# A macaron block on one core: expert weights copied to a ring and held stationary, biases off TensorE, attention on both row halves with its maxima and query masks on VectorE

## The chip, the core and the metric

The kernel runs on one core of a Trainium2 chip. A core has five engines that run their own instruction streams and meet only through semaphores: TensorE (PE) multiplies matrices and transposes, VectorE (DVE) and ScalarE (ACT) work element by element, GpSimd (POOL) does here a few element-wise steps and issues the indirect DMAs, and SyncE (SP) issues the plain ones. The on-chip memory has 128 partitions; TensorE writes into eight banks of a second memory, from which VectorE and ScalarE read.

The metric is the device time of one launch in microseconds (us), a median over runs.

## The reference

`x` holds 16 sequences of 256 tokens with 128 channels, so 4096 token rows. Everything is float32.

```
x = x + 0.5 * ffn(layernorm(x))
x = x + attention(layernorm(x))
x = x + 0.5 * ffn(layernorm(x))

ffn:   logits = x @ Wg.T + bg                      # 16 experts
       top 2 of them, softmax over the two -> cw
       gu = x @ Wgu[e] + bgu[e]                    # 128 -> 256
       gate, up = gu[::2], gu[1::2]                # min(gate, 7), clip(up, -7, 7)
       gated = (up + 1) * gate * sigmoid(1.702 * gate)
       out = sum over the two: cw * (gated @ Wd[e] + bd[e])

attention: q, k, v = split(x @ W_attn + b_attn), 16 heads of 8
       att = softmax(causal(q @ k.T / sqrt(8)));  y = att @ v
       y @ W_proj + b_proj
```

Both ffn use the same weights. The reference computes all 16 experts and masks; the kernel computes the chosen two.

## The kernel before, in words

**Stages.** The program runs once through: first router, first expert stage, attention with its projections, second router, second expert stage, output. Lines are those of the kernel before.

**Router.** It works on eight groups of four row tiles (512 tokens each, q = 0 to 7). For each: statistics (L853), variances, and one GpSimd power that turns variances into 1/std (the "root", L519). In the first router the root comes twice: for groups 0 and 1 before the first scatter, and one of 24 columns for groups 2 to 7 behind it. Then follow the normalised rows, transposes (L1287) and logits (L1295) on TensorE, the choice of two (L904), the ranks within each expert (L1307 to L1312), the positions (L932), and eight indirect DMAs on GpSimd that scatter the rows into a table sorted by expert (L528), 64 in all. A small table then says which expert each tile of 128 rows belongs to.

**Experts.** 80 tiles of 128 sorted rows are worked in 40 duos of two tiles (10 turns of 4 duos). Step functions are run at fixed distances behind each other: `turn_x` (L1355) transposes the rows, `gate_up` (L1364, L1365) multiplies, `turn_g` (L1373) transposes the gated result, `down` (L1384, L1385) multiplies again. Each product has a second one in front of it, of 3 rows, that adds the bias as three bf16 parts. The token rows are the stationary operand, and the expert's weights are the moving one, addressed through a register that TensorE loads from the tile table. ScalarE evacuates `xT` (L677), the sigmoid (L682), `gT` (L688) and `ysb` (L695); VectorE makes the gate in three operations (L1057, L1059, L1061) after one small one for the targets (L1054); GpSimd stores each duo with two indirect DMAs (L560).

**Attention.** 16 sequences times 4 groups of 4 heads are 64 units; 16 units make a turn of the loop. In unit s TensorE runs `scores(s+2)`, `max_T(s+1)`, `weights(s)` and `weigh_values(s-1)`.

- `scores` first writes the causal mask into the banks (L1125, L1128), then adds 12 products q·k (L1132, L1138), which use 64 of the 128 rows of the array: those of one head slot.
- VectorE takes the row maxima by two reductions (L762, L763), splits them into three bf16 parts (L765 to L771); `max_T` (L1146) transposes them.
- `weights` spreads the negated maxima over the keys (L1158, L1159, `select`), adds the mask (L1161, L1163) and forms the transposed products k·q (L1167, L1171); ScalarE takes the exponential (L594).
- `weigh_values` (L1191) multiplies with the values and a column group of ones, so that each head's denominator comes out beside it. Its two column halves of the array are used by neighbouring products.
- In two of each four units VectorE divides (reciprocal L779 on 128x256 elements, two multiplications L783); in the fourth `project_out` (L1199, L1200) follows and the residual is added (L789). Every eight units there are the projections to q, k and v of the next pair of sequences (L1096 to L1108), the splitting into bf16 parts (L753), the combination of the expert results (L715), and DMAs that stack the parts.

The last turn of attention also carries the first six groups of the second router; groups 6 and 7 come after it.

**What sets the order.** Each engine has its own program with the same sequence of steps; there is no planner. The class `Steps` (L1399) says which extra step falls in which unit, and `expert_pipeline` (L1469) how far the expert steps lie apart. On TensorE `scores` waits until the maxima of the unit two before are finished (`a_max`), since both use banks 0 to 2.

## Time and profile before

| | us |
|---|---|
| median of 3 runs | 1057.16 |
| lowest, highest | 1048.26, 1139.39 |
| span of the profiled execution | 1057.0 |

| engine | busy us | share of the span | instructions |
|---|---|---|---|
| TensorE, products | 842.6 | 80% | 5146 |
| TensorE, weight loads | 524.2 | 50% | 5147 |
| VectorE | 523.3 | 50% | 1733 |
| ScalarE | 283.7 | 27% | 537 |
| GpSimd | 338.3 | 32% | 346 |

A share of busy time is a mean over stages that have different limits, so the span is read in stretches: 0 to 118 first router, 118 to 351 first expert stage, 351 to 389 the way into attention, 389 to 709 its first 48 units, 709 to 786 the last turn up to the first scatter of the second router, 786 to 888 the rest of the last turn, the scatters and the tile table, 888 to 1028 the second expert stage, 1028 to 1057 output.
### The profile page before, as it was taken

How to read it: one execution, taken by the hardware profiler on the slowest of the kernel's cores; microseconds unless marked ns; L12 is line 12 of the kernel's file. 1: busy time of each engine (PE TensorE's matmuls, PEld its weight loads, DVE VectorE, ACT ScalarE, POOL GpSimd, SP SyncE). 2: the span in 40 equal slices, each digit the busy share in tenths (PEclk: the TensorE clock that was granted, in tenths of full speed). 3: DMA queues.
4: the chain of work that ended last, by engine and by line, in shares of the span. 5: the costliest groups of instructions: out<-in, count | busy, mean ns of one | idle time of the engine just before them, and what ended most of it. 6: DMA issues, size and time to landing. Idle time of an engine off the chain costs nothing.

```text
span 1057.0 us, 16653 instructions
## 1 busy us (share of the span) xinstructions
PE 842.6 (80%) x5146; PEld 524.2 (50%) x5147; DVE 523.3 (50%) x1733; ACT 283.7 (27%) x537; POOL 338.3 (32%) x346
## 2 busy tenths in 40 slices
PE   2240599999999249999999999999999633999970
PEld 1230255555555125666566656665666421555540
DVE  6571112212222245867586648677598650333326
ACT  1120122222222003333333223333233211334430
POOL 2677533333333201010101010102115672565560
PEclk9999999999999999998899789989598855999985
DMA  7026111111110152241324114223101125232217
GB/s 232 31 65 95 48 48 48 45 47 47 45 47 27 55 179 89 93 137 45 99 83 143 37 48 134 93 68 103 58 12 39 46 61 74 78 81 80 80 55 238
DMA packets 83348, 82.77 MB, mean 78 GB/s; under 512 B 10374, under 2 KB 74332, under 8 KB 83164
## 3 DMA queue, kind: packets, MB, share of 16 engines
q1 hardware_dynamic: 68508, 55.69, 18.2%
q0 software_dynamic: 10368, 23.15, 7.2%
q10 hardware_dynamic: 4416, 3.16, 1.4%
q8 instruction: 39, 0.64, 0.3%
q14 instruction: 17, 0.14, 0.0%
HBM read 41.92 MB, written 39.99 MB: 78 GB/s over the span
## 4 chain that ended last, share of the span: by engine, by line
PE 69%; DVE 10%; POOL 9%; issue 5%; DMA 4%; ACT 1%; SPq 1%; DVEq 0%; POOLq 0%; ACTq 0%
PE banks L1365 14%; PE banks L1385 8%; PE banks L1191 8%; POOL rows_by_expert L528 7%; PE banks L1364 4%; PE banks L1167 3%; PE banks L1158 3%; PE banks L1384 3%; PE banks L1138 3%; PE banks L1355 2%; PE banks L1373 2%; PE banks L1132 2%; PE banks L1125 2%; PE banks L1161 2%; PE banks L1102 2%
## 5 line engine op out<-in xcount | busy, mean ns | idle before, releaser
L560 POOL DMA_INDIRECT results_by_token<-ysb,goes_to x160 | 153.1, 957 | 221.4 <-ACT ysb L695 193.4
L1054 DVE TENSOR_TENSOR goes_to<-xt,konst_sb 128x2 int32<-128x2 f32 x80 | 12.9, 161 | 308.3 <-ACT sig L682 308.3
L1365 PE MATMUL banks<-w_experts,xT 128*128 x320 | 155.8, 580 | 0.0
L594 ACT ACTIVATE pT<-banks 128x1536 f32<-128x1536 f32 x64 | 92.8, 1451 | 121.1 <-PE banks L1171 121.1
L1191 PE MATMUL banks<-pT,values_spread 128*64 128x256 f32 (+1 forms) x1024 | 113.7, 367 | 0.0
L1385 PE MATMUL banks<-w_experts,gT 128*128 x320 | 103.4, 416 | 0.0
L1191 PEld LDWEIGHTS banks<-pT,values_spread 128*64 128x64 f32 x1024 | 81.0, 150 | 34.9 <-issue 18.8
L528 POOL DMA_INDIRECT rows_by_expert<-values_spread,posi x80 | 77.5, 969 | 40.5 <-issue 23.2
L1355 PE MATMUL banks<-konst_sb,xt 128*128 128x128 f32 x160 | 41.8, 355 | 59.1 <-DMA xt<-rows_by_expert 59.1
L762 DVE TENSOR_REDUCE mraw<-banks 128x4 f32<-128x512 f32 x64 | 44.2, 691 | 79.5 <-PE banks L1146 68.8
L1365 PEld LDWEIGHTS banks<-w_experts,xT 128*128 128x128 f32 x320 | 64.8, 253 | 27.9 <-issue 18.9
L763 DVE TENSOR_REDUCE mraw<-banks 128x4 f32<-128x1024 f32 x64 | 77.7, 1215 | 0.0
L1385 PEld LDWEIGHTS banks<-w_experts,gT 128*128 128x128 f32 x320 | 64.4, 251 | 14.8
L682 ACT ACTIVATE sig<-banks 128x256 f32<-128x256 f32 x80 | 30.6, 383 | 151.6 <-PE banks L1365 151.6
L496 POOL CAST q_parts<-sig 128x512 bf16<-128x512 f32 x7 | 4.2, 604 | 201.7 <-DVE sig L753 201.7
L588 ACT ACTIVATE mT<-banks 12x256 bf16<-12x256 f32 x64 | 23.8, 373 | 151.7 <-PE banks L1146 151.7
L779 DVE RECIPROCAL rsum<-ysum 128x256 f32<-128x256 f32 x34 | 59.4, 1747 | 1.1 <-ACT ysum L601 1.1
L1355 PEld LDWEIGHTS banks<-konst_sb,xt 128*128 128x128 f32 x160 | 28.0, 189 | 60.6 <-issue 58.6
L695 ACT ACTIVATE ysb<-banks 128x256 f32<-128x256 f32 x80 | 30.7, 383 | 96.5 <-PE banks L1385 96.5
L1364 PE MATMUL banks<-bias,ones 3*128 x160 | 53.9, 337 | 0.0
L1158 PE MATMUL banks<-mT,select 12*128 12x256 bf16 x256 | 53.7, 286 | 0.0
L1287 PE MATMUL banks<-konst_sb,values_spread 128*128 128x128 f32 x40 | 11.1, 433 | 49.8 <-DVE values_spread L879 49.8
(180 smaller groups left out, 1429.1 us busy)
## 6 DMA issues: line engine op xcount, KB each, us to landing
xt<-rows_by_expert SPq DMA_DIRECT2D x160, 64.5 KB, 1.9
q_stack<-q_by_part SPq DMA_DIRECT2D x8, 1024.0 KB, 7.2
k_stack<-k_by_part SPq DMA_DIRECT2D x8, 1024.0 KB, 7.2
q_by_part<-q_parts SPq DMA_DIRECT2D x16, 384.0 KB, 3.3
k_by_part<-k_parts SPq DMA_DIRECT2D x16, 384.0 KB, 2.8
yg<-results_by_token POOLq DMA_DIRECT2D x8, 512.0 KB, 5.0
results_by_token<-ysb,goes_to POOLq DMA_INDIRECT x160, 2.2
x_resident<-in_x SPq DMA_DIRECT2D x8, 256.0 KB, 5.3
```

The costliest lines, as they stand in the source:

```text
L528: pool.indirect_dma_start(out=rows_dram, out_offset=bass.IndirectOffsetOnAxis(ap=posi[:, c:c + 1], axis=0), in_=rows_of(f, q)[:, i, k, :], ...
L560: pool.indirect_dma_start(out=results_dram, out_offset=bass.IndirectOffsetOnAxis(ap=goes_to[:, 2 * k + i:2 * k + i + 1], axis=0), in_=ysb[ ...
L594: nc.scalar.activation(pT[:, s % 2, :], banks[:, 3:6, :].rearrange("p a q -> p (a q)"), ACT.Exp, scale=SCALE).then_inc(a_exp, 1)
L762: ch.mark(nc.vector.tensor_reduce(mraw[:, 0, :], bank[0][:, :].rearrange("p (g k) -> p g k", g=GRP), AX.X, ALU.max))
L763: ch.mark(nc.vector.tensor_reduce(mraw[:, 1, :], banks[:, 1:3, :].rearrange("p a (g k) -> p (a g) k", g=2), AX.X, ALU.max))
L779: ch.mark(nc.vector.reciprocal(rsum[:, c], ysum[:, c]))
L1158: nc.tensor.matmul(bank[3 + g // 2][:, g % 2 * T:(g % 2 + 1) * T], select[:, g, :], mT[:, s % 2, :], start=g % 2 == 0, stop=False)
L1191: last = nc.tensor.matmul(bank[6][r:r + HALF, c + kt * P:c + T], of_head, w, start=j == 0 and g < 2 and kt == 0, stop=j == GRP - 1 and g > ...
L1355: last = nc.tensor.transpose(bank[k % 2][:, i * P:(i + 1) * P], xt[:, 2 * k + i, 0:C], ident)
L1364: nc.tensor.matmul(o, ones[0:3, :], bias3[:, bass.ds(e[i], 2 * F)], start=True, stop=False)
L1365: last = nc.tensor.matmul(o, xT[:, k % 2, i * P:(i + 1) * P], w_all[:, bass.ds(e[i], 2 * F)], start=False, stop=True)
L1385: last = nc.tensor.matmul(o, gT[:, k % 2, i * P:(i + 1) * P], w_all[:, bass.ds(e[i] + 2 * F, C)], start=False, stop=True)
```

## The change

**Experts.** ScalarE copies the 384 weight columns of each tile's expert to a ring (`w_tile`, eight places) by an address from a register. TensorE reads fixed addresses, holds the weights (64 columns at a time) and streams the tokens, so `gate_up` gives the result already transposed: `turn_g` and its evacuation are gone. `down` runs in row halves of its output. The 3-row bias products are gone: `evac_x` adds 1.0 to each value, and during the first router `column_sums` and `adjust` change the weights once so that the added ones yield the bias; the bias of `down` is added by VectorE as it evacuates the result, which takes that evacuation from ScalarE. The steps lie further apart: in one slot ScalarE and TensorE work on four duos instead of three.

**Attention.** A head's rows are chosen so that neighbouring groups use different halves of the rows (`slot_of`). `scores` has no mask products. The maxima are taken by eight `tensor_tensor_reduce` that add the mask and reduce, and they are split into two parts instead of three. `scores` now waits for the eight (`a_read`), not for the end of the split. Since two halves of the rows may not write one bank at the same time, `scores` and `weights` wait once in between (`a_s_low`, `a_st_low`). `weigh_values` runs on quarters of the columns. The division is done once for each sequence on 32 denominators: `tokens_first` (4 transposes), a reciprocal of 128x32, one multiplication, `channels_first` (2 transposes), an evacuation by ScalarE, then `project_out` with its bias as one product.

**First router.** The roots come in four groups (`GROUPS`): quads 0, 1, and 2 to 3 before the first scatter, 4 to 7 (16 columns) behind it.

```diff
-EARLY = 2
+GROUPS = ((0, 1), (1, 2), (2, 4), (4, 8))
...
+                def copy_weights(t, k):
+                    n = t * DUOS + k + f * PAIRS
...
+                    beyond_first(act, s_y, n - (DUOS - 1))
+                    for i in range(2):
+                        last = nc.scalar.activation(w_tile[:, 2 * k + i, :], w_all[:, bass.ds(experts[key][k % 2 * 2 + i], EW)], ACT.Identity)
+                    last.then_inc(s_w, 1)
...
-                expert_pipeline(act, evac_x, sigmoid, evac_g, evac_y)
+                expert_pipeline(act, (1, evac_x), (2, sigmoid), (0, copy_weights))
...
+                ch.mark(nc.vector.memset(spare[:, :], 0.0))
+                for g in range(GRP):
+                    for qt in range(QT):
+                        of = bank[0][:, g * P:(g + 1) * P] if qt == 0 else bank[1 + g % 2][:, g // 2 * T:(g // 2 + 1) * T]
+                        lag = kc[:, K_MQ:K_MQ + P] if qt == 0 else kc[:, K_Z:K_Z + T]
+                        last = nc.vector.tensor_tensor_reduce(masked[:, (3 * g + qt) * P:(3 * g + 2 * qt + 1) * P], of, lag, 1.0, NEG * NEG_BELOW, ALU.add, ALU.max, mraw[:, s % 2, qt, g:g + 1])
+                        last.then_inc(a_read, 1)
...
-                ch.mark(nc.vector.tensor_reduce(mraw[:, 0, :], bank[0][:, :].rearrange("p (g k) -> p g k", g=GRP), AX.X, ALU.max))
-                ch.mark(nc.vector.tensor_reduce(mraw[:, 1, :], banks[:, 1:3, :].rearrange("p a (g k) -> p (a g) k", g=2), AX.X, ALU.max))
...
+                ch.mark(nc.vector.reciprocal(rsum[:, :], by_head[:, :, D]))
...
-                ch.mark(nc.vector.reciprocal(rsum[:, c], ysum[:, c]))
...
+                def evac_y(t, k):
+                    e = offsets(t, k)
...
+                    ch.mark(nc.vector.tensor_copy(goes_to[:, 2 * k:2 * k + 2], going[:, 2 * k:2 * k + 2]))
...
+                    for i in range(2):
+                        last = nc.vector.tensor_tensor(ysb[:, k, i, :], bank[6 + k % 2][:, i * C:(i + 1) * C], w_all[:, bass.ds(e[i] + EW, C)], ALU.add)
...
+                expert_pipeline(dve, (2, gate), (4, evac_y), (1, targets), chain=(ch, 3))
...
-                beyond_first(pe, a_max, n)
+                beyond_first(pe, a_read, n * 2 * GRP)
...
-                nc.tensor.matmul(bank[0].rearrange("p (g k) -> p g k", g=GRP), identb[:, :],
-                                 mask_q[:, :].unsqueeze(1).to_broadcast([P, GRP, P]), start=True, stop=False)
...
+                late(1)
+                early(0)
+                early(2).then_inc(a_s_low, 1)
+                late(3)
+                late(0)
+
+                pe.wait_ge(a_s_low, n + 1)
+                early(1)
+                late(2)
+                early(3).then_inc(a_s, 1)
...
+                    for i in range(2):
+                        o, e = bank[6 + n % 2][:, i * 2 * F:(i + 1) * 2 * F], 2 * n + i
+                        nc.tensor.matmul(o, share[0:3, :], bias3[0:3, e * BW:e * BW + 2 * F], start=True, stop=False)
+                        last = nc.tensor.matmul(o, spread[:, :], w_all[:, e * WB:e * WB + 2 * F], start=False, stop=True)
...
+                    for i in range(2):
+                        for which in range(2):
+                            for h in range(2):
+                                at = which * 2 * P + i * P
+                                last = nc.tensor.matmul(bank[2 + k % 2][h * HALF:(h + 1) * HALF, at:at + P],
+                                                        w_tile[:, 2 * k + i, which * F + h * HALF:which * F + (h + 1) * HALF],
+                                                        xT[:, k % 2, i * P:(i + 1) * P], start=True, stop=True)
...
-                expert_pipeline(pe, turn_x, gate_up, turn_g, down)
+                expert_pipeline(pe, (1, turn_x), (2, gate_up), (4, down))
```

The order of TensorE's instructions in the expert loop, before. One duo's share: `turn_g`, `turn_x`, `gate_up`, `down`; ISA rows with a matrix product's line are its register-addressed preparation.

```order
L1373 MATMUL banks<-konst_sb,upc 128x128 [waits s_gated]
L1373 MATMUL banks<-konst_sb,upc 128x128
...
L1355 MATMUL banks<-konst_sb,xt 128x128 [waits s_xt1,s_xt0]
L1355 MATMUL banks<-konst_sb,xt 128x128
...
L1364 ISA [waits s_xT]
L1364 MATMUL banks<-bias,ones 128x256
L1365 ISA
L1365 MATMUL banks<-w_experts,xT 128x256
...
L1384 ISA [waits s_ysb3,s_gT]
L1384 MATMUL banks<-bias,ones 128x128
L1385 ISA
L1385 MATMUL banks<-w_experts,gT 128x128
```

And after the change. `L1487` is `turn_x`, `L1500` is `gate_up`, `L1512` is `down`.

```order
L1487 MATMUL banks<-konst_sb,xt 128x128 [waits s_xt1,s_xt0]
L1487 MATMUL banks<-konst_sb,xt 128x128
L1492 REGISTER_ALU
L1599 REGISTER_ALU [waits s_xT,s_w]
L1500 MATMUL banks<-xT,pT 64x128 [waits s_gated]
L1500 MATMUL banks<-xT,pT 64x128 x7
L1512 MATMUL banks<-pT,row_buf 64x128 [waits s_ysb3,s_gated]
L1512 MATMUL banks<-pT,row_buf 64x128 x3
```

`turn_g`, the 3-row products and the register-addressed weights are gone; eight products of 64 columns stand in place of two of 128 with their bias, and a wait on the copied weights (`s_w`) is new.

TensorE's order in an attention unit, before: `scores`, `max_T`, `weights`, `weigh_values`.

```order
L1125 MATMUL banks<-mask_q,identb 128x512 [waits a_max]
L1128 MATMUL banks<-mask_q,identb 128x2x128 x2
L1132 MATMUL banks<-k_stack,q_stack 128x128 x4
L1138 MATMUL banks<-k_stack,q_stack 128x128 x8
L1146 MATMUL banks<-identb,mparts 12x128 [waits a_max,a_k_rest]
L1146 MATMUL banks<-identb,mparts 12x128
L1158 MATMUL banks<-mT,select 128x256 [waits a_exp,a_mT]
L1159 MATMUL banks<-mT,select 128x128
...
L1161 MATMUL banks<-mask_k,identb 128x2x128 x2
L1163 MATMUL banks<-mask_k,identb 128x512
L1167 MATMUL banks<-q_stack,k_stack 128x256 x4
L1171 MATMUL banks<-q_stack,k_stack 128x128 x4
L1191 MATMUL banks<-pT,values_spread 64x256 [waits a_exp,a_mT]
```

And after. `L1193` and `L1199` are the products of `scores`, `L1218` is `max_T`, `L1234` and `L1238` spread the maxima, `L1243` and `L1247` are the products of `weights`, `L1293` is `weigh_values`.

```order
L1199 MATMUL banks<-k_stack,q_stack 128x256 [waits a_read]
L1193 MATMUL banks<-k_stack,q_stack 128x128 x2
L1199 MATMUL banks<-k_stack,q_stack 128x256 x2
L1193 MATMUL banks<-k_stack,q_stack 128x128 [waits a_s_low]
L1199 MATMUL banks<-k_stack,q_stack 128x256
L1193 MATMUL banks<-k_stack,q_stack 128x128
L1218 MATMUL banks<-identb,mparts 64x128 [waits a_max,a_k_rest]
L1218 MATMUL banks<-identb,mparts 64x128 x3
L1234 MATMUL banks<-mT,select 128x256 [waits a_exp,a_mT]
L1238 MATMUL banks<-mT,select 128x128 x2
...
L1293 MATMUL banks<-pT,by_token 32x256 [waits a_exp]
L1293 MATMUL banks<-pT,by_token 32x256 x3
L1293 MATMUL banks<-pT,by_token 32x128 x4
```

The two mask rows ahead of the scores are gone, the wait `a_max` has become `a_read`, the scores are 8 products in place of 12, and a wait on `a_s_low` stands between the fifth and the sixth.

VectorE's order for the row maxima of a unit, before.

```order
L762 TENSOR_REDUCE mraw<-banks 128x4 [waits a_mTp,a_s]
L763 TENSOR_REDUCE mraw<-banks 128x4
L765 CAST mparts<-mraw 128x2x4 [waits s_vec]
L767 TENSOR_TENSOR mrest<-mraw,mparts 128x8 [waits s_vec]
L769 CAST mparts<-mrest 128x2x4 [waits s_vec]
L771 TENSOR_TENSOR mparts<-mrest,mparts 128x2x4 [waits s_vec]
```

And after (five more pairs of `L799` are left out).

```order
L794 MEMSET spare 128x1 [waits a_s]
L799 ISA by_token,mraw<-banks,konst_sb 128x128
L799 ISA mraw 128x1
L799 ISA by_token,mraw<-banks,konst_sb 128x256
L799 ISA mraw 128x1
...
L799 ISA by_token,mraw<-banks,konst_sb 128x256
L799 ISA mraw 128x1
L804 CAST mparts<-mraw 128x2x4 [waits a_mTp,a_read]
L806 TENSOR_TENSOR mparts<-mraw,mparts 128x2x4 [waits s_vec]
```

Two reductions have become eight instruction pairs, each a main one and a read of its accumulated value, and the four small operations of the split have become two.

## Rows read from the trace of the kernel before

**Rows 1.** Stages by windows: stretch, length, busy time per engine (count), PEclk, DMA share, GB/s.

```profile
118.00:351.00 233.00, 227.88 (x640) 125.71 (x640) 50.07 (x160) 60.67 (x160) 82.11 (x82) 1.00 0.16 44
389.00:709.00 320.00, 307.93 (x2597) 199.61 (x2596) 220.05 (x518) 105.97 (x129) 31.20 (x35) 0.93 0.27 88
709.00:786.00 77.00, 74.08 (x605) 49.57 (x604) 56.99 (x193) 24.53 (x31) 8.57 (x7) 0.84 0.17 56
786.00:888.00 102.00, 58.57 (x494) 41.50 (x493) 62.44 (x259) 23.32 (x31) 63.69 (x65) 0.73 0.25 54
888.00:1028.00 140.00, 135.71 (x640) 79.94 (x640) 50.11 (x160) 53.27 (x160) 75.53 (x79) 0.95 0.27 74
```

**Rows 2.** Groups by line, 160 to 300 (first expert stage): line, engine, names, count | busy, mean | idle.

```profile
L1365 PE MATMUL banks<-w_experts,xT 128*128 x100 | 61.1, 715 | 0.0
```

**Rows 3.** Chain that ended last, 118 to 351, its shares by line.

```profile
by line: PE banks L1365 39.5%; PE banks L1385 23.7%; PE banks L1364 11.1%; PE banks L1355 7.2%; PE banks L1384 7.0%; PE banks L1373 7.0%; DMA results_by_token<-ysb,goes_to 1.9%; issue 1.3%; POOL results_by_token L560 1.2%; DMA xt<-rows_by_e
```

**Rows 4.** Groups by line, 920 to 1000 (second expert stage).

```profile
L560 POOL DMA_INDIRECT results_by_token<-ysb,goes_to x50 | 47.9, 957 | 33.7 <-ACT ysb L695 23.9 <-issue 9.8
L1365 PE MATMUL banks<-w_experts,xT 128*128 x100 | 35.0, 432 | 0.0
```

**Rows 5.** Chain that ended last, 480 to 495: start, us, what; one attention unit.

```profile
483.54 2.81 PE banks L1191 x16
...
491.20 1.50 PE banks L1191 x16
```

**Rows 6.** Timeline of PE, 440 to 447: start, us, line, operands, count; one unit.

```profile
440.97 0.39 PE L1125 MATMUL banks<-mask_q,identb 128*128 128x512 bf16 x1
...
441.51 0.40 PE L1132 MATMUL banks<-k_stack,q_stack 64*128 64x128 bf16 x4
...
442.29 0.28 PE L1146 MATMUL banks<-identb,mparts 128*12 128x128 bf16 x2
442.50 0.28 PE L1158 MATMUL banks<-mT,select 12*128 12x256 bf16 x1
...
443.26 0.39 PE L1161 MATMUL banks<-mask_k,identb 128*128 128x256 bf16 x2
...
446.06 0.39 PE L1125 MATMUL banks<-mask_q,identb 128*128 128x512 bf16 x1
```

**Rows 7.** Groups by line, DVE, 389 to 709 (48 attention units).

```profile
L763 DVE TENSOR_REDUCE mraw<-banks 128x4 f32<-128x1024 f32 x48 | 58.3, 1214 | 0.0
L779 DVE RECIPROCAL rsum<-ysum 128x256 f32<-128x256 f32 x23 | 40.2, 1747 | 0.0
L762 DVE TENSOR_REDUCE mraw<-banks 128x4 f32<-128x512 f32 x48 | 33.2, 692 | 69.6 <-PE banks L1146 59.2 <-PE banks L1138 9.2 <-issue 0.3
...
L715 DVE SCALAR_TENSOR_TENSOR x_resident<-yg,wts,x_resident 128x128 f32 x48 | 13.7, 348 | 0.9 <-DVE x_resident L715 0.9
```

**Rows 8.** Timeline of DVE, 950 to 954: the gate's operations on one duo.

```profile
951.88 0.16 DVE L1054 TENSOR_TENSOR goes_to<-xt,konst_sb 128x2 int32<-128x2 f32 x1 [1.98 <-ACT sig L682]
951.96 0.42 DVE L1057 SCALAR_TENSOR_TENSOR sig<-banks,sig 128x256 f32<-128x256 f32 x1
952.30 0.41 DVE L1059 TENSOR_SCALAR upc<-banks 128x256 f32<-128x256 f32 x1
```

**Rows 9.** Timeline of POOL, 30 to 46 (first router).

```profile
31.42 4.21 POOL L519 TENSOR_TENSOR rstd<-veps,neghalf 128x24 f32<-128x24 f32 x1
42.20 1.03 POOL L528 DMA_INDIRECT rows_by_expert<-values_spread,posi  x1 [6.57 <-DVE posi L942]
43.53 0.96 POOL L528 DMA_INDIRECT rows_by_expert<-values_spread,posi  x1 [0.30 <-issue]
```

**Rows 10.** Timeline of POOL, 780 to 890 (the second router's longest wait).

```profile
814.61 0.96 POOL L528 DMA_INDIRECT rows_by_expert<-row_buf,posi  x1 [8.27 <-DVE posi L942]
```

**Rows 11.** DMA issues of the page: operands, queue, count, KB each, us to landing.

```profile
k_stack<-k_by_part SPq DMA_DIRECT2D x8, 1024.0 KB, 7.2
...
k_by_part<-k_parts SPq DMA_DIRECT2D x16, 384.0 KB, 2.8
```

445 lines of the change are left out of this document (260 added, 185 removed).

## The prediction

> **What bounds the kernel now.** I read the page's shares first, then the windows by stage, the groups by line in each, the timeline of one unit and the chain of waits. The windows [rows 1] show TensorE as the limit: it is busy for 228 of 233 us in the first expert stage, 308 of 320 in the first 48 attention units, 74 of 77 after them, and 136 of 140 in the second expert stage. Only 786 to 888 is different: 64 of 102 us are GpSimd's, which scatters one DMA each 0.96 + 0.30 = 1.26 us [rows 9], 10.1 us for a group's eight.
>
> The reader should see one more thing. The window of the first expert stage gives a granted clock of 1.00, yet the same product takes 715 ns there and 432 ns in the second stage [rows 2, 4], a ratio of 1.66. The record of the clock doesn't fit the durations. I take the first stage as run at 1.2 GHz and the second at 2.4 GHz, though TensorE was no less busy in the first. In attention both levels occur: the same `weigh_values` takes 2.81 us and, one unit later, 1.50 [rows 5].
>
> The page's span is 1057.0 us and the median 1057.16, so the sum against the one is a sum against the other.
>
> **Start: −7.** The 24-column root takes 4.21 us, and the next scatter comes at 42.20 after 6.57 us of waiting [rows 9]; scatters are back to back from there. With 16 columns behind the first group (by columns about 2.9 us) and the others already done, it can start near 35. Column sums and the eight additions on VectorE fall in the last four groups, of which each has 10.1 us of scatters as cover; without it they'd cost some 8 us (8 times the 1 us of an addition plus its product, estimate).
>
> **First expert stage: −83.** A duo takes 233/40 = 5.83 us. The chain by line [rows 3] divides it: products with weights 63.2%, 3-row products 18.1%, two sets of transposes 7.2 and 7.0%, 4.5% other. After: 12 products of 128 columns into 64 rows, 1536 columns, which is what a unit's `weigh_values` is (four of 256, four of 128), also float32, also in alternate column halves: 2.81 us at the low clock [rows 5]. With one set of transposes (7.2% of 5.83 = 0.42) and the other 4.5% (0.26) a duo is 3.5 us; 40 of them and 10 for filling a pipeline of four steps are 150. Others stay below: GpSimd needs 2 x 1.26 = 2.52 for its stores, VectorE about 2.5 (three gate operations at 0.34 to 0.42 [rows 8], two operations of 0.16, two additions near 0.3, a register load), ScalarE about 1.8 (two of 0.38, two copies of near 0.5). The copy waits for the `down` of four duos before; behind it on ScalarE's queue stand `evac_x` and the sigmoid, which have a slot in hand.
>
> **Second expert stage: −21.** At the high clock TensorE needs 1.50 [rows 5] + 0.25 (0.42 divided by 1.66) + 0.26 = 2.0 us, so GpSimd's 2.52 and VectorE's 2.5 decide. I take 2.7 (before it was 3.2, with GpSimd idle 33.7 of 80 us for results [rows 4]). 40 x 2.7 + 11 (about 10 us of start at the low clock, as before) = 119 against 140.
>
> **First 48 attention units: −70.** Now 320/48 = 6.67 us each. The bare unit at the high clock is 446.06 − 440.97 = 5.09 [rows 6]; the other 1.58 is projections, output products and stretches at the low clock. On TensorE the score masks go (0.54); scores, spread maxima and products of `weights` (0.78, 0.76, about 0.76) halve if the two row halves run together, about −1.15; changes of shape cost perhaps 0.2. That leaves 3.6, and 4.7 with a low-clock share of 0.45 taken out of the 1.58 and the rest in.
>
> So the loop across VectorE and TensorE decides: `scores` must wait until the eight maxima have read the banks, and the maxima for the scores. No row shows a `tensor_tensor_reduce`. Lower bound: reductions over the same 1536 columns, 692 + 1214 ns [rows 7], and 0.08 for each of six more (from 951.88 to 951.96, the start of an operation of two columns to that of the next [rows 8]), 2.4 us. Upper bound: 0.35 for 128 columns [rows 7], 0.43 for 256, 0.16 (an operation on two columns [rows 8]) for each accumulator read, 4.4 us. I take 3.1: four at the streamed 0.34 us for 256 columns, from 951.96 to 952.30 [rows 8], which is the nearest row in kind, four at 0.25, and eight reads at 0.09. With 0.65 for the scores and 0.15 of latencies the loop is 3.9 us.
>
> On top, in eight units VectorE has about 9 us of other work (combination 8 x 0.35 [rows 7], statistics, normalising, two splits of 0.75 twice, additions; the divisions shrink from 1747 ns twice in four units to well under 1), of which 1.2 lies beside the scores. That gives 4.9, and 0.3 for low-clock stretches where TensorE is the limit: 5.2, or 250 us for 48.
>
> The Trainium skill (VectorE: DVE Perf Modes, the section on the DRAIN) says that after each operation the pipe empties for about its duration less 266 ns before the next begins. By it the eight would come to about 3.6 us and the stage to −46. The trace here starts the next operation 0.34 us after one of 0.42 us, so it doesn't agree, and I keep my value.
>
> The parts are still stacked in time: 2.8 us and 7.2 us of DMA [rows 11] and about 3 of casts are 13 us, against four units or 20 us.
>
> **Last turn −15, scatters −8.** In 709 to 786 TensorE is busy 74 of 77 us at a clock of 0.84 [rows 1]; by the ratio 5.2/6.67, less for the router's own steps, it becomes 62. Behind it GpSimd sets the pace of 81 us for 64 scatters; the 21 us left of the stretch are waits for positions, the longest 8.27 us [rows 10], and the tile table; the waits shrink with shorter units but don't vanish, and I take 8.
>
> Two more waits are new on TensorE (`a_s_low`, `a_st_low`). Behind each stand products only of the same unit and their bank's other half; they cost the emptying of the array, in the 0.2 above. Sending the divisions through TensorE adds six transposes in four units, at about 0.13 us (half of the 0.25 of the two in an expert duo) 0.2 a unit: TensorE's 4.7 becomes 4.9, level with VectorE's. So nothing is left as cover there, and whatever TensorE needs beyond this is added in full.
>
> Sum: −7 − 83 − 21 − 70 − 15 − 8 = −204 and −1 for the way into attention; 1057 − 205 = **852 us**.
>
> **Rivals.**
>
> *The first expert stage gets the high clock too.* TensorE's work per duo would be 2.0 us and the stage 119 instead of 150: 821. For it: TensorE will be as busy as in the second stage, which had the high clock. Against: it was busy 98% of the first stage before and stayed low [rows 1, 2]. 18%. The Trainium skill (TensorE: Matmul & The Clock Gate, Part 1) says that sustained activity releases the throttle; by that rule this rival would be the forecast. The first stage's row speaks against it.
>
> *The second stage stays low as well.* 150 instead of 119: 883. TensorE would idle a quarter of each duo there. 10%.
>
> *The row halves don't run together*: the change doesn't do what it says in attention. No row of before has alternate row halves; column halves do it. TensorE then keeps 4.75 of the bare unit plus 1.35, 6.1 per unit: 0.9 x 58 more, 904. 9%.
>
> *Attention falls to the low clock*, because TensorE now waits each unit for VectorE. A low unit of before is 491.20 − 483.54 = 7.66 [rows 5], less 0.54 of masks 7.1: 1.9 x 58 more, 962. 8%.
>
> *The maxima run at a slow rate* (the other side). The reciprocal needs 1747 ns for 256 columns, 6.8 ns each [rows 7]. If the combined add and reduce did so, eight would take 10.5 us, a unit 12.4, and the time would be near 1270. It is slower than before from 3.1 + 205/58 = 6.6 us for the eight, 0.83 each. For it: a new instruction form with two tensors, and its accumulator read. Against: all other operations with two tensors here run near 1.3 ns per column (0.34 us for 256). 5%.
>
> **The numbers.** Forecast 852, 48%; with the rivals 98%, and 2% for anything else. The measurement can tell about 2% from no change. The forecast's own range is 830 to 890: the bounds of the maxima are −0.7 and +1.3 us in 58 units, −41 and +75, and each end goes about half way to them, since below TensorE holds the unit near 4.9 and above the row of 0.34 us speaks against it. From 795 to 920 the range takes in the first three rivals and leaves out the low clock in attention, the slow maxima and the tails. Faster: the first five cases and half of the rest, 94%. Slower: the slow maxima but for 1% near the break-even, 4%. Within 2%: that and the other half, 2%.
>
> **What would show it.** First expert stage: near 150 us, products of 64 rows at about 0.23 us each. Second: GpSimd's idle time before its stores gone. In attention: unit starts 5.2 us apart, VectorE without idle time but for the scores, and TensorE waiting for `a_read`; eight maxima within 3.1 us. The last root with 16 columns and the next scatter near 35. The prediction fails if a maximum takes over 0.6 us, or if scores of alternate halves start no closer together than those of one half.

## The result, and the profile after

The changed kernel takes 784.08 us (782.61 to 784.66, 4 runs); the kernel before, run beside it, stood at 1094.61 (1048.26 to 1139.39). The ratio is 0.745, interval 0.741 to 0.749. The forecast was 852 us with a range from 795 to 920: the direction was right, and the time lies 11 us under the range. Runs of before lie near 1050 or near 1143 us (once 959.09), and the ratio is taken against those near 1050: the trace at 1057 has the second expert stage at TensorE's high clock, and the same loop in a trace at 1138.63 (b_burst) has it at the low clock like the first.

The profiled execution has a span of 782.8 us. The windows of its stages, in the columns of [rows 1]:

```profile
105.00:223.00 118.00, 83.92 (x1040) 61.79 (x1040) 74.97 (x281) 63.46 (x160) 80.37 (x82) 0.94 0.31 90
260.00:493.00 233.00, 194.77 (x2481) 112.29 (x2481) 175.35 (x1094) 108.71 (x140) 31.29 (x35) 0.88 0.36 121
493.00:551.00 58.00, 47.81 (x603) 28.96 (x604) 47.58 (x314) 25.62 (x36) 8.53 (x8) 0.91 0.22 74
551.00:638.00 87.00, 43.60 (x481) 28.23 (x481) 49.92 (x323) 23.55 (x33) 63.24 (x65) 0.71 0.27 61
638.00:755.00 117.00, 84.63 (x1040) 61.68 (x1040) 75.35 (x281) 63.62 (x160) 77.05 (x81) 0.89 0.31 91
```

The stages, cut at the same events in both traces (last scatter, last store, first maxima of units 0 and 48, first scatter of the second router), against the terms of the forecast:

| stretch | before | after | difference | forecast |
|---|---|---|---|---|
| start to last scatter | 113.2 | 104.7 | −8.5 | −7 |
| first expert stage, to its last store | 237.8 | 118.5 | −119.3 | −83 |
| on to the first maxima | 38.2 | 36.4 | −1.8 | −1 |
| 48 attention units | 320.2 | 233.3 | −86.9 | −70 |
| last turn to first scatter | 76.7 | 58.0 | −18.7 | −15 |
| scatters | 96.1 | 87.2 | −8.9 | −8 |
| second expert stage, to its last store | 147.1 | 117.0 | −30.1 | −21 |
| output | 27.7 | 27.7 | 0 | 0 |

The forecast's windows began at 118 and 888 us, 5 to 6 us behind the last scatters, so its lengths of these stages are shorter than those here by about that much; the differences can be compared. They sum to −274.2, which is 1057.0 − 782.8. Two thirds of the 69 us by which the forecast missed stand in the expert stages, most of the rest in attention.

**Expert stages.** The groups of lines from 130 to 200, columns as in [rows 2, 4]:

```profile
L582 POOL DMA_INDIRECT results_by_token<-ysb,goes_to x56 | 53.9, 963 | 17.1 <-issue 15.6 <-DVE ysb L1128 1.5
L1500 PE MATMUL banks<-xT,pT 128*64 128x128 f32 x480 | 32.8, 278 | 4.9 <-DVE row_buf L1100 4.7
```

A product of 64 columns has a mean of 278 ns in the first stage. Its start in the timeline of TensorE (start, us, line, operands, count) shows the change of level:

```profile
113.44 1.98 PE L1500 MATMUL banks<-xT,pT 128*64 128x128 f32 x16
...
115.97 1.13 PE L1500 MATMUL banks<-xT,pT 128*64 128x128 f32 x16
```

The same 16 records take 1.98 us at 113.44 and 1.13 us at 115.97; the granted clock has a recorded rise at 116.1. These are the products of the first and of the second duo, so the stage enters at 1.2 GHz and runs at 2.4 GHz from its second duo on, though TensorE is busy for only 83.9 of its 118 us. Then GpSimd paces it: the first store comes at 122.15, the last ends at 223.2, 80 stores in 101.1 us or 1.26 each. The second stage has nearly the same, 101.2 us, from 653.96 to 755.1.

**Attention.** One unit on TensorE and the maxima of one unit on VectorE, as timelines:

```profile
299.95 0.86 PE L1293 MATMUL banks<-pT,by_token 128*32 128x256 f32 x16
300.75 0.28 PE L1199 MATMUL banks<-k_stack,q_stack 64*128 64x256 bf16 x1
300.75 0.28 PE L1193 MATMUL banks<-k_stack,q_stack 64*128 64x128 bf16 x2
...
301.31 0.30 PE L1218 MATMUL banks<-identb,mparts 128*64 128x128 bf16 x4
301.55 0.28 PE L1234 MATMUL banks<-mT,select 64*128 64x256 bf16 x1
...
302.34 0.39 PE L1269 MATMUL banks<-mask_k,identb 128*128 128x256 bf16 x2
...
303.10 0.86 PE L1293 MATMUL banks<-pT,by_token 128*32 128x256 f32 x16
303.89 0.28 PE L1312 MATMUL banks<-bias,ones 3*128 3x256 bf16 x1
...
304.69 0.28 PE L1199 MATMUL banks<-k_stack,q_stack 64*128 64x256 bf16 x1
```

```profile
297.78 0.28 DVE L799 CUSTOM_DVE_ANT_0 by_token<-banks,konst_sb 128x128 f32<-128x128 f32 x1 [0.65 <-issue]
...
297.99 0.08 DVE L799 DVE_READ_ACCUMULATOR2_ANT mraw<- 128x1 f32 x1
297.99 0.42 DVE L799 CUSTOM_DVE_ANT_0 by_token<-banks,konst_sb 128x256 f32<-128x256 f32 x1
298.33 0.08 DVE L799 DVE_READ_ACCUMULATOR2_ANT mraw<- 128x1 f32 x1
298.33 0.28 DVE L799 CUSTOM_DVE_ANT_0 by_token<-banks,konst_sb 128x128 f32<-128x128 f32 x1
...
300.00 0.08 DVE L799 DVE_READ_ACCUMULATOR2_ANT mraw<- 128x1 f32 x1
...
301.44 0.29 DVE L799 CUSTOM_DVE_ANT_0 by_token<-banks,konst_sb 128x128 f32<-128x128 f32 x1 [0.20 <-issue]
```

Products of `scores` on different row halves start in the same hundredth of a microsecond (300.75). The scores take 301.31 − 300.75 = 0.56 us, and with the transposes, the spreading and the products of `weights` it is 302.34 − 300.75 = 1.59 us up to the masks; before, scores, transposes and spreading alone took 443.26 − 441.51 = 1.75 [rows 6]. The Trainium skill (TensorE: Matmul & The Clock Gate, Part 3) says that products in different row groups run at the same time with starts within some 4 ns; the trace agrees. `weigh_values` on column quarters takes 303.89 − 303.10 = 0.79 us, where it took 1.50 [rows 5]. The eight maxima take from 297.78 to 300.08, 2.30 us: a new one starts every 0.21 (128 columns) or 0.34 us (256), and each read of an accumulator starts together with the next operation, so it adds nothing that shows to the 0.34 us that a two-tensor operation of 256 columns takes in [rows 8].

TensorE is busy for 194.77 of the 233 us of this window. Its longest waits in it (engine, line, released by: us in total, times, longest):

```profile
PE banks L1218 <- DVE x_resident L820: 20.3, 6, 3.4
...
PE banks L1199 <- DVE mraw L799: 5.9, 3, 2.4
```

Only 5.9 us are the wait of `scores` for the maxima. 20.3 us, and 7.2 more of the same kind behind the splitting for q and k, are waits of `max_T` (L1218) in the units in which VectorE has other work.

**First router.** The last root and the first scatter of the second group (GpSimd's timeline), the answer to [rows 9]:

```profile
30.92 3.17 POOL L540 TENSOR_TENSOR rstd<-veps,neghalf 128x16 f32<-128x16 f32 x1
34.15 1.06 POOL L549 DMA_INDIRECT rows_by_expert<-by_token,posi  x1
35.51 0.96 POOL L549 DMA_INDIRECT rows_by_expert<-by_token,posi  x1 [0.30 <-issue]
```

### The profile page after: what moved, and what is told of

Same layout as the page of the kernel before. It is cut to its first block, busy times and chain, and to the rows that moved or that the text cites. A ratio compares the mean times of both kernels' runs of the same rounds, so it can differ in the third digit from the quotient of the medians.

```text
span 782.8 us, 19236 instructions
## 1 busy us (share of the span) xinstructions
PE 514.2 (66%) x5867; PEld 328.6 (42%) x5867; DVE 512.6 (65%) x2750; ACT 300.9 (38%) x554; POOL 334.5 (43%) x348
## 4 chain that ended last, share of the span: by engine, by line
DVE 23%; POOL 23%; PE 23%; issue 22%; DMA 4%; ACT 3%; DVEq 2%; SPq 1%; POOLq 0%; ACTq 0%
POOL results_by_token L582 12%; POOL rows_by_expert L549 10%; DVE by_token L799 5%; PE banks L1293 2%; DVE x_resident L1140 2%; PE banks L1243 2%; PE banks L1269 2%; DVE x_resident L749 2%; PE banks L1420 2%; PE banks L1218 2%; PE banks L1168 1%; PE banks L1161 1%; PE banks L1271 1%; PE banks L1234 1%; DVE upc L1098 1%
## 5 line engine op out<-in xcount | busy, mean ns | idle before, releaser
L799 DVE CUSTOM_DVE_ANT_0 by_token<-banks,konst_sb 128x128 f32<-128x128 f32 (+1 forms) x512 | 147.1, 352 | 38.3 <-issue 38.1
L717 ACT ACTIVATE pT<-w_experts 128x384 f32 x160 | 74.9, 516 | 69.7 <-DMA tab<-tabc 42.8
L1500 PE MATMUL banks<-xT,pT 128*64 128x128 f32 x1280 | 90.0, 284 | 10.4 <-DVE row_buf L1100 9.0
L549 POOL DMA_INDIRECT rows_by_expert<-by_token,posi x80 | 77.0, 963 | 28.5 <-issue 23.2
L1500 PEld LDWEIGHTS banks<-xT,pT 128*64 128x64 f32 x1280 | 70.7, 140 | 27.5 <-DVE row_buf L1100 16.5
L1487 PE MATMUL banks<-konst_sb,xt 128*128 128x128 f32 x160 | 35.6, 306 | 46.6 <-DMA xt<-rows_by_expert 45.9
L1512 PE MATMUL banks<-pT,row_buf 128*64 128x128 f32 x640 | 52.9, 285 | 15.5 <-DVE ysb L1128 13.1
L1293 PE MATMUL banks<-pT,by_token 128*32 128x256 f32 (+1 forms) x1024 | 59.6, 354 | 0.0
L1199 PE MATMUL banks<-k_stack,q_stack 64*128 64x256 bf16 x256 | 42.4, 288 | 22.1 <-DVE mraw L799 13.5
L1512 PEld LDWEIGHTS banks<-pT,row_buf 128*64 128x64 f32 x640 | 37.1, 139 | 27.7 <-issue 24.5
L1243 PE MATMUL banks<-q_stack,k_stack 64*128 64x256 bf16 x256 | 44.5, 294 | 0.0
L1234 PE MATMUL banks<-mT,select 64*128 64x256 bf16 x256 | 44.0, 296 | 0.0
L1293 PEld LDWEIGHTS banks<-pT,by_token 128*32 128x32 f32 x1024 | 28.1, 116 | 34.8 <-issue 25.0
L1218 PE MATMUL banks<-identb,mparts 128*64 128x128 bf16 x256 | 20.7, 245 | 33.6 <-DVE x_resident L820 20.3
L1487 PEld LDWEIGHTS banks<-konst_sb,xt 128*128 128x128 f32 x160 | 16.6, 145 | 61.7 <-issue 58.1
```

Source lines behind the costliest of these rows:

```text
L549: pool.indirect_dma_start(out=rows_dram, out_offset=bass.IndirectOffsetOnAxis(ap=posi[:, c:c + 1], axis=0), in_=rows_of(f, q)[:, i, k, :], ...
L717: last = nc.scalar.activation(w_tile[:, 2 * k + i, :], w_all[:, bass.ds(experts[key][k % 2 * 2 + i], EW)], ACT.Identity)
L799: last = nc.vector.tensor_tensor_reduce(masked[:, (3 * g + qt) * P:(3 * g + 2 * qt + 1) * P], of, lag, 1.0, NEG * NEG_BELOW, ALU.add, ALU. ...
L1199: return nc.tensor.matmul(bank[1 + g % 2][:, c:c + T], q[r, pair, m, o + P:o + T], k[r, pair, m, o:o + T], start=g // 2 == 0, stop=g // 2 ...
L1234: nc.tensor.matmul(bank[3 + g % 2][:, g // 2 * T:(g // 2 + 1) * T], select[maxima(g), g, :], mT[maxima(g), s % 2, :], start=g // 2 == 0, s ...
L1243: nc.tensor.matmul(bank[3 + g % 2][:, c:c + T], k[r, pair, m, o:o + P], q[r, pair, m, o:o + T], start=False, stop=False)
```

## The experiments

All edits start from one of the two kernels. Times of a stage come from the same events as in the table.

**Is the first stage of before slow because it enters at the low clock?** First a burst of dense products ahead of the loop:

```diff
+                    pe.wait_ge(s_asetup, 5)
+                    for _ in range(30):
+                        nc.tensor.matmul(bank[5].rearrange("p (g k) -> p g k", g=GRP), identb[:, :],
+                                         identb[:, :].unsqueeze(1).to_broadcast([P, GRP, P]), start=True, stop=True)
```

> The kernel before with 30 dense products of 512 columns (bf16, identity by identity) on TensorE directly ahead of the first expert loop; nothing else is changed. They take about 13 us at 1.2 GHz, less if they are granted the high clock. Theory H (history): the loop of before holds whichever clock it enters with, and the first expert stage was slow only because it entered at the low level; then the same product takes 432 ns instead of 715, the stage is near 140 us instead of 233 and the whole about 80 us shorter. Theory F (form): the loop's own instructions (products of 3 rows, transposes, short gaps) keep the clock low or let it fall again; then the products are 715 ns after the burst, at the latest some 10 us on, and the whole is 5 to 13 us longer.

1137.04 us (1047.71 to 1140.99). It decided nothing: the burst ran beside the loading of the first tiles, the clock rose at 100.8 and fell at 111.1, and the loop began at 118 at the low level. A burst that ends before the work is no test of what the work inherits. So it was moved behind the loop's first wait:

```diff
+                    if f == 0 and k == 0 and isinstance(t, int) and t == 0:
+                        pe.wait_ge(s_asetup, 5)
+                        for _ in range(40):
+                            nc.tensor.matmul(bank[5].rearrange("p (g k) -> p g k", g=GRP), identb[:, :],
+                                             identb[:, :].unsqueeze(1).to_broadcast([P, GRP, P]), start=True, stop=True)
```

> The kernel before with 40 dense products of 512 columns (bf16) on TensorE directly ahead of the first transposes of the first expert loop, behind its wait for the first tiles; in b_burst the burst ran while the tiles were still being loaded, and TensorE stood still for 12 us before the loop. They take 10 to 17 us. Theory H (history): the loop of before holds the clock that it enters with, and its first stage was slow only because it entered low: the products behind the burst take 432 ns, the stage some 140 us instead of 233, the whole about 80 us less. Theory F (form): the loop itself lets the clock fall: products of 715 ns again some 10 to 30 us into it, the whole 10 to 17 us more.

1063.49 us (1054.59 to 1073.60), 80 less than the 1143 that both stages at the low clock take. Its timeline and its stages (columns of the windows as in [rows 1]; the second one holds the second stage):

```profile
118.09 10.24 PE L1357 MATMUL banks<-identb 128*128 128x512 bf16 x40 [36.81 <-DMA xt<-rows_by_expert]
...
129.31 0.70 PE L1370 MATMUL banks<-w_experts,xT 128*128 x2
```

```profile
121.00:261.00 140.00, 138.41 (x674) 80.98 (x672) 49.99 (x160) 52.57 (x159) 75.87 (x79) 1.00 0.26 70
753.00:1032.00 279.00, 236.55 (x682) 132.32 (x682) 68.59 (x259) 64.65 (x167) 106.44 (x111) 0.50 0.20 49
```

```profile
L1370 PE MATMUL banks<-w_experts,xT 128*128 x160 | 97.7, 715 | 0.0
```

Behind the burst two records of the weight product take 0.70 us, and the high clock stays from 121.0 to 261.0, to the end of the stage, which is 3.27 us per duo instead of 5.68. In the same execution the second stage, which had no burst, stayed at 0.50, with a product of 715 ns, and needed 5.68 us per duo. So theory H holds for the high level: entered at 2.4 GHz, the loop kept it for 140 us with the 3-row products in it. For the low level it holds less firmly, as before's own second stage shows:

```profile
888.00:891.00 3.00, 2.26 (x7) 1.18 (x7) 0.00 (x0) 0.77 (x2) 0.00 (x0) 0.50 0.50 112
...
897.00:900.00 3.00, 3.00 (x14) 1.55 (x13) 1.65 (x7) 1.07 (x3) 0.00 (x0) 0.93 0.18 44
900.00:904.00 4.00, 4.00 (x23) 2.44 (x22) 1.95 (x7) 1.81 (x6) 1.92 (x2) 1.00 0.21 49
```

It entered at 0.50 too, and the clock rose at 897.4, 9 us into the loop, ahead of its first `down` at 899. The second stage of b_burst2 began in the same way and did not rise. What decides between the two no run shows. In each trace the level that a stage reaches in its first ten microseconds stays until TensorE's work in it thins out (in the changed kernel at 208.2).

**What kept it from rising?** The bias products taken out of before:

```diff
-                        nc.tensor.matmul(o, ones[0:3, :], bias3[:, bass.ds(e[i], 2 * F)], start=True, stop=False)
                         last = nc.tensor.matmul(o, xT[:, k % 2, i * P:(i + 1) * P], w_all[:, bass.ds(e[i], 2 * F)],
-                                                start=False, stop=True)
+                                                start=True, stop=True)
...
-                        nc.tensor.matmul(o, ones[0:3, :], bias3[:, bass.ds(e[i] + 2 * F, C)], start=True, stop=False)
```

> The kernel before without the 3-row bias products of both expert stages (the biases of gate, up and down are left out of the result). Theory F: the 3-row products keep the first loop at 1.2 GHz; without them it gets 2.4 GHz, products of 432 ns, the stage falls from 233 to 110 to 120 us (GpSimd's 2.52 to 2.7 us per duo) and the second stage from 140 to about 115. Theory H: the clock stays low in the first stage, a duo is 5.83 less 18% = 4.8 us, the stage 190, and only the second gains the rest: about 65 us less in all.

904.50 us (897.71 to 908.40), some 148 less than a run of before near 1052.

```profile
113.00:229.00 116.00, 88.24 (x480) 68.44 (x480) 50.16 (x160) 55.99 (x160) 86.31 (x83) 0.98 0.34 91
267.00:582.00 315.00, 301.91 (x2606) 196.33 (x2605) 220.41 (x519) 106.23 (x130) 31.20 (x35) 0.91 0.28 90
760.00:876.00 116.00, 87.57 (x480) 67.95 (x480) 50.07 (x160) 56.17 (x160) 77.27 (x81) 0.93 0.33 91
```

```profile
L560 POOL DMA_INDIRECT results_by_token<-ysb,goes_to x63 | 61.2, 971 | 19.2 <-issue 15.6 <-ACT ysb L695 3.7
L1364 PE MATMUL banks<-w_experts,xT 128*128 x126 | 34.7, 397 | 4.5 <-issue 3.7
```

The clock rises at 125.1, and the stores of each stage take 101.6 and 101.3 us, as in the changed kernel. Attention takes 6.55 us per unit, against 6.67. So register-addressed moving weights, the transposes of the gated result and three evacuations on ScalarE, all of which this kernel still has, cost the expert stages nothing that shows: with the 3-row products gone they are already at GpSimd's pace. The converse, the four products back in the changed kernel:

```diff
+                        nc.tensor.matmul(bank[4][:, 0:2 * F], ones[0:3, :], bias3[0:3, 0:2 * F], start=True, stop=True)
...
+                        nc.tensor.matmul(bank[4][:, 0:C], ones[0:3, :], bias3[0:3, 0:C], start=True, stop=True)
```

> The changed kernel with the four 3-row products of before put back in front of each duo's products (256, 256, 128 and 128 columns, into a bank that nobody reads), in both expert stages. Theory F: products that use 3 of 128 rows keep the clock at 1.2 GHz; then a duo is 3.5 + 1.06 = 4.6 us in the stages that stay low, 80 us more for each such stage, 80 to 165 in all. Theory H or the dense form of the new products being what counts: the clock rises as in the changed kernel, a duo needs 2.0 + 0.5 = 2.5 us on TensorE, level with GpSimd's 2.52, and the whole is 0 to 15 us more.

982.10 us (980.66 to 983.65): 198 more, and above what either theory gave.

```profile
106.00:321.00 215.00, 201.95 (x1200) 108.47 (x1200) 75.28 (x281) 63.54 (x160) 79.95 (x82) 1.00 0.17 50
738.00:951.00 213.00, 201.94 (x1200) 108.47 (x1200) 75.52 (x281) 63.59 (x160) 76.65 (x81) 0.50 0.17 50
```

```profile
L1501 PE MATMUL banks<-xT,pT 128*64 128x128 f32 x192 | 27.1, 434 | 0.0
...
L1497 PE MATMUL banks<-bias,ones 3*128 3x256 bf16 x24 | 9.3, 389 | 0.0
```

Both stages took 5.05 us per duo with a product of 434 ns: the low level. (My 4.6 was 0.45 short; whether the 3.5 us of the other products or the 1.06 us of the 3-row ones was too low, no run separates.) The two windows are alike to the microsecond in TensorE's busy time, yet the column of the granted clock says 1.00 in the first and 0.50 in the second. That settles how to read the 1.00 in [rows 1]: the column shows full speed until the first recorded change, here at 370.8, whatever the engine ran at. And was it their 3 rows, or the extra work?

```diff
-                        nc.tensor.matmul(bank[4][:, 0:2 * F], ones[0:3, :], bias3[0:3, 0:2 * F], start=True, stop=True)
+                        nc.tensor.matmul(bank[4][:, 0:2 * F].rearrange("p (a k) -> p a k", a=2), identb[:, :], select[:, 0:2, :], start=True, stop=True)
...
-                        nc.tensor.matmul(bank[4][:, 0:C], ones[0:3, :], bias3[0:3, 0:C], start=True, stop=True)
+                        nc.tensor.matmul(bank[4][:, 0:C], identb[:, :], select[:, 0, :], start=True, stop=True)
```

> The same as a_rows3, but the four extra products per duo use all 128 rows of the array (identity by a bf16 table) instead of 3, with the same columns, the same count and the same place. a_rows3 took 982 us, with 5.05 us per duo at the low clock in both expert stages. If it is the 3 of 128 rows that hold TensorE at 1.2 GHz, both stages get the high clock here, GpSimd paces them again at 2.52 us per duo, and the whole is 784 to 800 us. If it is the extra products as such (time and columns between the others), the stages stay low and the time is 970 to 990 us.

817.19 us (814.23 to 818.38), 165 less than with 3 rows.

```profile
118.00:234.00 116.00, 114.66 (x1175) 69.54 (x1173) 74.94 (x278) 60.60 (x153) 73.05 (x76) 1.00 0.28 82
668.00:784.00 116.00, 113.43 (x1160) 68.74 (x1158) 74.19 (x275) 59.58 (x150) 73.93 (x77) 1.00 0.28 83
```

```profile
L1501 PE MATMUL banks<-xT,pT 128*64 128x128 f32 x328 | 27.0, 285 | 0.0
...
L1497 PE MATMUL banks<-select,identb 128*128 128x256 bf16 x41 | 11.4, 278 | 0.0
```

The clock rises at 118.0, the product takes 285 ns, a duo 2.93 us with TensorE busy for 114.66 of 116. The same number of products with the same columns at the same places lets the clock rise when they use 128 rows and does not when they use 3, in both stages of either run. (The edit also adds a wait for the two tables ahead of the loop, and the operands' values differ too; no run has the same values, or a number of rows between 3 and 128.) Over all the traces here, the ten kernels without 3-row products rise in all 20 stages, and the four with them in one of seven stages entered low. The 33 us over the changed kernel are 80 duos of 2.93 instead of 2.53.

**What paces the expert stages now?** ScalarE's copies cut to 8 columns after the first turn of each stage:

```diff
-                        last = nc.scalar.activation(w_tile[:, 2 * k + i, :], w_all[:, bass.ds(experts[key][k % 2 * 2 + i], EW)], ACT.Identity)
+                        last = nc.scalar.activation(w_tile[:, 2 * k + i, 0:wide], w_all[:, bass.ds(experts[key][k % 2 * 2 + i], wide)], ACT.Identity)
```

> The changed kernel with ScalarE copying the full 384 weight columns only in the first turn of each expert stage and 8 columns afterwards (later tiles so use the weights of the first eight). My theory: both expert stages are paced by GpSimd's two indirect DMAs per duo (2.52 us), so taking 1.0 us of ScalarE per duo away changes nothing, within 1%. Rival: ScalarE's copies and the register loads in front of them are in the cycle of a slot (the copy waits for the down products, evac_x stands behind it), then each stage loses up to 10 us.

785.51 us (783.80 to 789.68), 1.4 more, which is within its spread: the copies cost nothing. One store per duo in the second stage:

```diff
-                        for i in range(2):
+                        for i in range(2 - f):
                             pool.indirect_dma_start(
```

> The changed kernel with one indirect store per duo instead of two in the second expert stage (half of its results are left out). If GpSimd's stores set the pace there (2.52 us per duo), the stage falls to the next limit: VectorE at about 2.2 to 2.5 us per duo, or TensorE at about 2.0 at the high clock; 5 to 20 us less. Rival: the pace is set by VectorE or ScalarE already and GpSimd only happens to be level; then nothing changes.

770.43 us (767.23 to 773.60), 13.7 less: 2.15 us per duo instead of 2.53.

```profile
POOL results_by_token L582 <- DVE ysb L1128: 32.8, 26, 1.7
```

GpSimd now waits for VectorE's evacuation in nearly each duo (32.8 of 60 us). Which engine is the next limit stays open: in 660 to 730 VectorE is busy for 59.6 of 70 us and TensorE for 62.9. GpSimd's stores pace the changed kernel's expert stages; the next step down is only 0.4 us per duo away.

**First router.**

```diff
-GROUPS = ((0, 1), (1, 2), (2, 4), (4, 8))
+GROUPS = ((0, 1), (1, 2), (2, 8))
```

> The changed kernel with the first router's last root of 24 columns again (quads 2 to 7) behind the first scatter instead of 16. My theory: the root of 16 columns took 2.8 us, that of 24 takes 4.2, and the second group of scatters stood at 34.2 instead of 42.2; the roots account for all of it, so this gives back 5 to 8 us. Rival: the earlier start is mostly VectorE's new order (statistics before the first scatter), and only the 1.4 us of the longer root and a wait for it come back.

794.32 us (793.25 to 797.70), 10.2 more. The second group of scatters begins at 41.60 again, and the last scatter ends at 112.9 instead of 104.7. These 8.2 us are nearly the whole gain of the router, 8.5, so it is the roots. The other 2 us lie in stages that the edit doesn't touch: the 48 units take 231.0 us here and the last turn 61.0.

**Attention.** One caution for small differences: in five runs whose attention is unchanged (a_nocopy, a_onestore, a_root24, a_rows3, a_rows128) the 48 units take 230.8 to 233.8 us, and 233.3 in the changed kernel. The reciprocals back on VectorE:

```diff
+                if s % GRP in (1, 2):
+                    nc.vector.reciprocal(filler[:, 1, :], filler[:, 0, :])
```

> The changed kernel with the reciprocal of 128x256 elements that before had in two of each four attention units (1.75 us each) put back on VectorE as an extra operation on other data. If VectorE paces attention (busy 184 of 244 us with the rest in the latency of its cycle with TensorE), 32 x 1.75 = 56 us come back but for what lies beside the scores (up to 0.8 us a unit, 26 us): 30 to 56 us more. Rival: TensorE paces most units now and VectorE has slack; then under 15 us more.

819.25 us (818.17 to 824.54), 35 more. The 48 units take 256.5 instead of 233.3: 0.48 us a unit of the 0.87 that were added.

```profile
262.00:518.00 256.00, 195.90 (x2488) 111.75 (x2489) 211.79 (x1118) 108.63 (x140) 31.27 (x35) 0.89 0.32 110
```

TensorE has the same busy time as in the changed kernel's window. TensorE's waits for the maxima grow from 5.9 to 18.3 us. The row halves apart, here in `scores` and in the same manner in `weights`:

```diff
-                late(1)
                 early(0)
                 early(2).then_inc(a_s_low, 1)
-                late(3)
                 late(0)
+                late(2)

                 pe.wait_ge(a_s_low, n + 1)
+                late(1)
+                late(3)
                 early(1)
-                late(2)
                 early(3).then_inc(a_s, 1)
...
```

> The changed kernel with the products of scores and weights in an order in which each half of the rows comes first as a whole (groups 0 and 2, then 1 and 3), so that neighbours use the same half; the same products, banks and waits. If the two halves run at the same time in the changed order, scores go from about 0.55 to 0.8 us and weights from 0.9 to 1.6, and of these the 0.3 us of the scores lie in the cycle of VectorE and TensorE: 15 to 50 us more in 64 units. If they don't run at the same time, or TensorE's time is covered, under 8 us.

820.96 us (819.23 to 822.04), 37 more; 5.49 us per unit instead of 4.86.

```profile
297.43 0.28 PE L1193 MATMUL banks<-k_stack,q_stack 64*128 64x128 bf16 x2
...
298.20 0.30 PE L1218 MATMUL banks<-identb,mparts 128*64 128x128 bf16 x4
298.44 0.28 PE L1238 MATMUL banks<-mT,select 64*128 64x128 bf16 x2
...
299.65 0.39 PE L1269 MATMUL banks<-mask_k,identb 128*128 128x256 bf16 x2
```

Up to the transposes of the maxima the scores take 298.20 − 297.43 = 0.77 us instead of 0.56, and `weights` up to its masks 299.65 − 298.44 = 1.21 instead of 302.34 − 301.55 = 0.79. That is about 0.63 more per unit, and 0.63 is what a unit became longer. The wait for the whole split, as before:

```diff
-                beyond_first(pe, a_read, n * 2 * GRP)
+                beyond_first(pe, a_max, n)
```

> The changed kernel with scores waiting, as before, for the end of the split of the maxima (a_max) instead of the eight reads of the banks (a_read). The split takes two operations of 0.17 us and their waits, 0.4 us from the last read. VectorE in the cycle: the scores start 0.4 us later in every unit where VectorE has nothing else to do meanwhile; up to 25 us more. Rival: other work of VectorE (divisions, combination) or TensorE's own order already stands in between: under 8 us.

789.79 us (788.67 to 790.23), 5.7 more: 1.6 in the 48 units, which is within the 3 us above, 1.5 in the last turn and the rest spread over the other stages, the expert stages too. So the wait costs under 8 us, as the rival said, and how much of the 5.7 is its own stays open. And the plain reductions:

```diff
+                nc.vector.tensor_reduce(mraw[:, s % 2, 0, :], bank[0][:, :].rearrange("p (g k) -> p g k", g=GRP), AX.X, ALU.max).then_inc(a_read, GRP)
+                nc.vector.tensor_reduce(mraw[:, s % 2, 1, :].rearrange("p (h a) -> p a h", a=2), banks[:, 1:3, :].rearrange("p a (g k) -> p a g k", g=2), AX.X, ALU.max).then_inc(a_read, GRP)
```

> The changed kernel with the eight combined add-and-reduce operations of a unit replaced by two plain reductions as before (of 512 and 1024 columns); the causal mask is left out of the maxima, so some results are off. They took 0.69 + 1.21 = 1.9 us where the eight take 2.3. If VectorE's time for the maxima lies in the cycle, 0.4 us a unit, 20 to 26 us less. Rival: the first reduction must wait for all scores in either case and TensorE paces: within 8 us.

778.41 us (776.39 to 780.16), 5.7 less; 4.71 us a unit, 0.15 less where VectorE had 0.4 less to do. That is within the rival's 8 us and far from my theory (20 to 26 less).

## Why the prediction was right or wrong

**First expert stage (−83, measured −119): the clock was wrong.** The step that failed is "I take the first stage as run at 1.2 GHz", carried over to the changed kernel. The reading of before was right: the durations of [rows 2, 4] and the alike windows of a_rows3 show it. What I made of it was not. I argued that TensorE was 98% busy and stayed low, so a busy engine would stay low again. The runs show that what the engine is busy with counts, and not the busy share alone: with four products of 3 rows per duo the changed loop, entered low, stays low at 94% busy in both stages; without them it rises at its second duo, in a stage in which TensorE is 71% busy, and with 128-row products in their place it rises as well. It is not a fixed rule, for before's second stage rose with the 3-row products in it; why it did stays open. The 5.83 us per duo were too long by a little as well: they hold the filling (from store to store a duo takes 5.68), and 10 us of filling were added again. The rival with 18% was this case. That its 119 us for the stage stand so near to 118.5 is luck: it counted 40 × 2.7 + 11 from a start 4.8 us behind the last scatter, and by that cut the stage took 113.8, with a pace of 2.53. The Trainium skill's rule (TensorE: Matmul & The Clock Gate, Part 1), that activity releases the throttle, stands for the changed loop, but not if activity is read as the busy share: before was 98% busy in its first stage and stayed low.

**Second expert stage (−21, measured −30).** The pace was GpSimd's 2.53 us, not 2.7, and the low start was shorter: the clock rises at 648.6, 3.9 us behind the first product with weights, where I had 10. The limit was named rightly, and so was that the weight copies are covered (a_nocopy). The sum counted on the ring, the stationary weights and the missing transposes to shorten TensorE's part of a duo; at the high clock that shortens nothing, for b_nobias reaches the same pace without them. What counts is that the bias products are gone. The filling is even 3 us longer in the changed kernel (17.5 us from last scatter to first store against 14.3 in b_nobias).

**Attention (−70, measured −87).** Two terms were mis-sized. The unit's `weigh_values` was kept at 1.50 us in the sum, though its split from halves to quarters of the columns is in the change; it takes 0.79. The maxima were put at 3.1 us, bounded below by 2.4, and took 2.30: the bound charged 0.08 us for each further instruction, and they overlap. The Trainium skill's rule on the pipe emptying after each VectorE operation (VectorE: DVE Perf Modes, the section on the DRAIN) would have given 3.6, further off. By these two a unit should have gained 0.7 to 1.5 us on 5.2, and it gained 0.34, because the bound was also misnamed. I had VectorE's cycle as the limit and TensorE waiting for `a_read`. The waits show 5.9 us of that in 48 units. In the timelines TensorE starts the next scores at 300.75, 0.67 us after the maxima have read the banks at 300.08: it was still at its own `weigh_values` (299.95). a_apart's 0.63 us on TensorE came through whole, a_recip's 0.87 us on VectorE for a little over half, a_reduce's 0.4 for 0.15. So TensorE's own sequence is on the path in the units where VectorE has little beside the maxima, and VectorE's in those where it has more: of TensorE's 38 us without work in the window, 33.6 end with VectorE, 27.7 of them before `max_T`, a wait that the forecast's cycle did not have; in the unit shown the maxima come 301.44 − 297.78 = 3.66 us apart, and the 4.86 is the mean with projections, combinations and stretches at the low clock.

**The rest.** That the row halves run together held, and would have cost 37 us otherwise (a_apart; forecast for that rival: 52). The router's −8.5 against −7 is the roots, as said; column sums and additions stayed under the scatters. The stacking DMAs stayed covered: TensorE waits for one of them only once, on the way into attention. The slow maxima did not occur: 0.29 us each on average, against the 0.83 from which it would have been slower.

## What to carry to other kernels

Read the clock from the durations of one product in two places, not from its column before the first recorded change. A product that uses few rows can cost more than its own time, for here it held the whole loop at the low clock in most stages entered low (198 us more in a_rows3, 33 with 128 rows in a_rows128); fold such a bias into the weights or the eviction. When an engine is named as the pace, ask for a run that adds to it and one that adds to its partner: only the part that comes through is on the path.

## What was not expected of the hardware

- Four 3-row products per duo, 18.1% of the chain in before's first stage [rows 3], can keep a loop entered at 1.2 GHz there to its end: 982.10 us with them, 817.19 us with 128-row products in their place. Before's loop, which has them, kept the high clock for 140 us where it started with it (b_burst2).
- The combined add and reduce runs at 0.34 us for 256 columns with its accumulator read hidden, start to start; a plain reduction of 1024 columns takes 1.21 us, 0.30 for 256. All eight take 2.30 us against 1.91 for the two plain reductions [rows 7]: the mask costs a fifth more, not a second pass.
- The products of `weigh_values` on four column quarters of 32 take 0.79 us for what takes 1.50 us on two halves of 64.
